# A state-space scan's read-outs summed and turned to token order in one step on TensorE

## The reference, cut to what matters

```
x = x + ssm(ctx, z=layernorm(x))       # z is read as (b, channel, time): the 256x256 of a sequence as it lies
x = x + ffn0(layernorm(x));  x = x + attention(layernorm(x), ctx);  x = x + ffn1(layernorm(x))

ssm:  u = silu(conv(in_proj_w @ ctx) + conv_b)          # 256 channels
      dt, B, C = x_proj_w @ u  (8, 16 and 16 rows);  delta = softplus(dt_proj_w @ dt + dt_proj_b)
      for every time t and state n:
          state[n] = state[n] * exp(delta * A[n]) + delta * u * B[n]
      y = sum_n state[n] * C[n]
      y = y + D * u
      y = y * silu(z)
      return y with channel and time swapped
```

## Time and profile before

| | before |
|---|---|
| median of 3 runs (lowest, highest) | 853.95 us (853.61, 855.42) |
| the profiled execution: its time, its span | 855.85 us, 853.9 us |
| TensorE matmul busy, share of the span | 728.4 us, 85% |
| VectorE busy | 600.3 us, 70% |
| ScalarE busy | 435.3 us, 51% |
| GpSimd busy | 292.6 us, 34% |
| mean granted TensorE clock | 0.909 |

### The profile page before, as it was taken

The page is one execution under the profiler, slowest core; times in us unless marked ns, Lnnn a source line. Parts: engine busy times, 40 slices in busy tenths (PEclk is TensorE's granted clock), DMA queues, the critical chain, the costliest instruction groups (busy, mean ns, idle before and its releaser), DMA issues.

```text
span 853.9 us, 10187 instructions
## 1 busy us (share of the span) xinstructions
PE 728.4 (85%) x3448; PEld 566.6 (66%) x3448; DVE 600.3 (70%) x1119; ACT 435.3 (51%) x836; POOL 292.6 (34%) x259
## 2 busy tenths in 40 slices
PE   5267636567868899999989999999899988999997
PEld 1012114345645678888789999998799876888886
DVE  6999986999999856645467566677656566455454
ACT  5555104555442354445467677766677645333342
POOL 0100321222233324445355555545354633212131
PEclk8575766888889999999989999999899999999999
DMA  6233321445354425455211111111111223433330
GB/s 178 98 107 103 113 78 55 114 131 165 121 167 113 124 74 172 148 163 162 70 53 41 34 59 32 50 44 33 26 51 56 75 79 99 144 117 101 103 130 25
DMA packets 40530, 81.33 MB, mean 95 GB/s; under 512 B 5752, under 2 KB 8064, under 8 KB 40480
## 3 DMA queue, kind: packets, MB, share of 16 engines
q1 hardware_dynamic: 40480, 80.69, 30.7%
HBM read 79.30 MB, written 1.38 MB: 94 GB/s over the span
## 4 chain that ended last, share of the span: by engine, by line
PE 56%; DVE 14%; issue 8%; ACT 4%; POOL 1%; DMA 0%; SPq 0%; DVEq 0%; ACTq 0%; POOLq 0%
PE bank L86 17%; PE bank L87 17%; PE bank L88 17%; PE bank L575 3%; DVE read_out L1030 3%; DVE state L1012 3%; DVE bank L1184 1%; DVE hidden_lo L914 1%; ACT probs L865 1%; DVE read_out L1038 1%; POOL probs L1429 1%; DVE bank L1187 1%; ACT w_hi L659 1%; PE bank L399 1%; DVE x_tok L1055 1%
## 5 line engine op out<-in xcount | busy, mean ns | idle before, releaser
L1376 POOL TENSOR_TENSOR w_lo<-w_raw,w_hi 128x768 fp32r<-128x768 f32 (+1 forms) x106 | 197.3, 1862 | 371.8 <-ACT w_hi L659 371.5
L86 PE MATMUL bank<-xt_hi,w_hi 128*128 128x512 f32 x400 | 169.2, 423 | 36.8 <-DVE hidden_lo L914 36.8
L659 ACT ACTIVATE w_hi<-w_raw 128x768 fp32r<-128x768 f32 (+1 forms) x106 | 85.7, 811 | 156.0 <-PE bank L88 125.0
L87 PE MATMUL bank<-xt_lo,w_hi 128*128 128x512 f32 x400 | 162.7, 407 | 0.0
L88 PE MATMUL bank<-xt_hi,w_lo 128*128 128x512 f32 x400 | 162.6, 407 | 0.0
L86 PEld LDWEIGHTS bank<-xt_hi,w_hi 128*128 128x128 f32 x400 | 77.9, 195 | 60.2 <-DVE hidden_lo L914 41.6
L659 ACT ACTIVATE hidden_hi<-bank 128x512 fp32r<-128x512 f32 x84 | 49.4, 588 | 121.7 <-DVE bank L1187 120.2
L369 PE MATMUL bank<-read_out,identity 128*128 128x512 f32 x96 | 64.0, 804 | 41.5 <-DVE read_out L1030 40.0
L914 DVE TENSOR_TENSOR hidden_lo<-bank,hidden_hi 128x512 fp32r<-128x512 f32 x84 | 57.8, 688 | 58.3 <-ACT hidden_hi L659 58.2
L1184 DVE TENSOR_TENSOR bank<-gated,bank 128x512 f32<-128x512 f32 x80 | 55.4, 692 | 50.7 <-PE bank L88 49.9
L88 PEld LDWEIGHTS bank<-xt_hi,w_lo 128*128 128x128 f32 x400 | 78.0, 195 | 19.3
(11 more groups left out here) (171 smaller groups left out, 1495.1 us busy)
## 6 DMA issues: line engine op xcount, KB each, us to landing
w_raw<-in_ffn_w SPq DMA_DIRECT2D x74, 384.0 KB, 3.3
b_rows<-bc_scratch SPq DMA_DIRECT2D x32, 256.0 KB, 3.6
c_rows<-bc_scratch SPq DMA_DIRECT2D x32, 256.0 KB, 3.2
route_bc<-route_scratch SPq DMA_DIRECT2D x32, 256.0 KB, 3.6
route_bc<-route_scratch SPq DMA_DIRECT2D x32, 192.0 KB, 3.3
w_raw<-in_attn_proj_w SPq DMA_DIRECT2D x16, 384.0 KB, 3.0
route_bc<-route_scratch SPq DMA_DIRECT2D x32, 128.0 KB, 3.7
w_raw<-in_attn_out_w SPq DMA_DIRECT2D x16, 256.0 KB, 2.6
```

The costliest lines, as they stand in the source:

```text
L86: e.matmul(out, w_hi, m_hi, start=first, stop=False)
L87: e.matmul(out, w_hi, m_lo, start=False, stop=False)
L659: e.activation(out, source, ACT.Copy).then_inc(sem(name), 1)
L1376: e.tensor_tensor(lo[:, 0:n], w_raw[p % RAW][:, 0:n], hi[:, 0:n].bitcast(F32), ALU.subtract).then_inc(sem("w_lo"), 1)
```

## The change

The sum over the states is made by transposes. `y_sum` now takes eight 128 x 128 blocks of a read-out and transposes each into bank 0 or 1 with accumulation, so that a bank holds one sequence in token order (2 x 128 tokens in turn, 256 channels), and y comes out turned. It runs once for each read-out in both halves; the pairs of half 1 are gone. D * u is made on ScalarE (`make_skip`) in slot 3 of `read_out` and is the first term of the sum (n = -1). z is transposed after it is normalised (`turn_z`, 16 transposes through banks 6 and 7), and silu reads it from PSUM into the place where z was, now in token order. After the sum VectorE multiplies the bank by z in place (`gate_y`) and adds it to x (`add_y`, which in half 1 follows in the same unit). `turn_y`, `add_pair` and `skip_and_gate` are gone.

```diff
--- before.py
+++ after.py
@@ -362,24 +362,30 @@
                     e.matmul(ps[:, :], dt_proj_sb[:, c * P:(c + 1) * P], x_dbl[0:DR, h * HT:(h + 1) * HT],
                              start=True, stop=True).then_inc(sem("dt"), 1)
 
-            def y_sum(h, n, tile, first):
-
-                for c in range(EH):
-                    ps = take(c, ("y_skip", 2 * h + c + 1)) if first else bank[c]
-                    last = e.matmul(ps[:, :], identity[:, :], tile[:, c, :], start=first, stop=n == DS - 1)
-                last.then_inc(sem(f"y_sum{h}"), 1)
-
-            def turn_y(h):
-                y = read_out[h]
+            def y_sum(h, n):
+
+                tile = read_out[3 if n < 0 else n % 4]
+                at.wait_ge(*(("skip", h + 1) if n < 0 else ("read", h * DS + n + 1)))
                 for b in range(HB):
-                    at.wait_ge("y_gated", 2 * h + b + 1)
-                    ps = misc(("y", h, b), ("y_added", 2 * h + b + 1))
+                    ps = take(b, ("y_added", 2 * h + b + 1)) if n < 0 else bank[b]
                     for l in range(SEQ // P):
                         for c in range(EH):
                             t = b * SEQ + l * P
-                            last = e.transpose(ps[:, l * DI + c * P:l * DI + (c + 1) * P], y[:, c, t:t + P],
-                                               identity[:, :])
-                    last.then_inc(sem("y_turn"), 1)
+                            last = e.matmul(ps[:, l * DI + c * P:l * DI + (c + 1) * P], tile[:, c, t:t + P],
+                                            identity[:, :], is_transpose=True, start=n < 0 and l + c == 0,
+                                            stop=n == DS - 1 and l + c == 2)
+                last.then_inc(sem(f"y_sum{h}"), 1)
+
+            def turn_z():
+
+                for b in range(BATCHES):
+                    at.wait_ge("z_norm", b // HB + 1)
+                    ps = take(6 + b % 2, ("z_gate", b + 1))
+                    for l in range(SEQ // P):
+                        for c in range(EH):
+                            last = e.transpose(ps[:, l * DI + c * P:l * DI + (c + 1) * P],
+                                               z_gate[:, b * EH + c, l * P:(l + 1) * P], identity[:, :])
+                    last.then_inc(sem("z_turn"), 1)
 
             def turn_acc(k, pair, ring=(0, 1)):
                 at.wait_ge("acc_copy0", k - 3)
@@ -478,14 +484,15 @@
             at.wait_ge("consts", 4)
             project_x_dbl(0)
             project_dt(0)
+            y_sum(0, -1)
             for n in range(DS):
-                at.wait_ge("read", n + 1)
-                y_sum(0, n, read_out[n % 4], n == 0)
+                y_sum(0, n)
+                if n == 1:
+                    turn_z()
                 if n == 2:
                     project_x_dbl(1)
                 if n == 6:
                     project_dt(1)
-            turn_y(0)
             for step in (5, 6, 7, 8, 11):
                 transition(2, step)
 
@@ -495,14 +502,8 @@
                 if u >= 2:
                     down(u - 2)
                 n = u + 1
-                if 2 < n < DS and n % 2 == 1:
-                    at.wait_ge("pair", (n - 1) // 2)
-                    y_sum(1, n - 2, read_out[(DS + 1 + n - 2) % 4], n == 3)
-                if n == DS + 1:
-                    at.wait_ge("pair", DS // 2)
-                    y_sum(1, DS - 1, read_out[(DS + 1 + DS - 1) % 4], False)
-                if n == DS + 2:
-                    turn_y(1)
+                if n <= DS + 1:
+                    y_sum(1, n - 2)
                 if n == DS + 4:
                     transition(3, 5)
                     transition(3, 6)
@@ -701,10 +702,21 @@
                                         ACT.Exp, scale=decay[:, c, n:n + 1])
                 last.then_inc(sem("decay"), 1)
 
-            def activate_z(h):
-                at.wait_ge("z_norm", h + 1)
-                z = z_gate[:, h * HC:(h + 1) * HC, :]
-                e.activation(z, z, ACT.Silu).then_inc(sem("z_gate"), 1)
+            def activate_z():
+                for b in range(BATCHES):
+                    at.wait_ge("z_turn", b + 1)
+                    e.activation(z_gate[:, b * EH:(b + 1) * EH, :].rearrange("p c s -> p (c s)"), bank[6 + b % 2][:, :],
+                                 ACT.Silu).then_inc(sem("z_gate"), 1)
+
+            def make_skip(h):
+
+                at.wait_ge("conv", 2 * HALVES)
+                if h > 0:
+                    at.wait_ge("y_sum0", DS + 1)
+                for c in range(EH):
+                    at.wait_ge("u", 2 * h + c + 1)
+                    last = e.activation(read_out[3][:, c, :], u_sb[:, h, c, :], ACT.Copy, scale=skip_d[:, c:c + 1])
+                last.then_inc(sem("skip"), 1)
 
             def round_weights(p):
                 if p >= PIECES:
@@ -786,12 +798,12 @@
             softplus_log(0)
             for n in range(4):
                 scan_decay(0, n)
+            make_skip(0)
             for n in range(DS):
                 if n + 4 < DS:
                     scan_decay(0, n + 4)
                 if n == 1:
-                    for h in range(HALVES):
-                        activate_z(h)
+                    activate_z()
                     for c in range(EH):
                         activate_u(1, c)
                 if n == 2:
@@ -804,6 +816,7 @@
                 round_weights(p)
             for step in (5, 6, 7, 8):
                 transition(2, step)
+            make_skip(1)
             for n in range(4):
                 scan_decay(1, n)
 
@@ -1016,39 +1029,20 @@
                 i = h * DS + n
                 at.wait_ge("state", i + 1)
                 at.wait_ge(f"ld_c{i % 3}", 16 * (i // 3 + 1))
-                if h == 0:
-                    slot = n % 4
-                    at.wait_ge("y_sum0", n - 3)
-                else:
-                    slot = (DS + 1 + n) % 4
-                    at.wait_ge("y_sum0", DS)
-                    if n == 3:
-                        at.wait_ge("y_turn", HB)
-                    elif n > 3:
-                        at.wait_ge("y_sum1", (n - 3) // 2)
-                        at.wait_ge("pair", (n - 2) // 2)
-                e.tensor_tensor(read_out[slot][:, :, :], state[i % 2][:, :, :],
+                at.wait_ge("y_sum0", n - 2 if h == 0 else DS + 1)
+                if h == 1:
+                    at.wait_ge("y_sum1", n - 2)
+                e.tensor_tensor(read_out[n % 4][:, :, :], state[i % 2][:, :, :],
                                 c_rows[i % 3][:, :].unsqueeze(1).broadcast_to([P, EH, HT]),
                                 ALU.mult).then_inc(sem("read"), 1)
 
-            def add_pair(n):
-
-                at.wait_ge("read", DS + n + 1)
-                both = read_out[(DS + 1 + n) % 4][:, :, :]
-                e.tensor_tensor(both, both, read_out[(DS + n) % 4][:, :, :], ALU.add).then_inc(sem("pair"), 1)
-
-            def skip_and_gate(h):
-                y = read_out[h]
-                at.wait_ge(f"y_sum{h}", DS if h == 0 else DS // 2)
-                for c in range(EH):
-                    e.scalar_tensor_tensor(out=y[:, c, :], in0=u_sb[:, h, c, :], scalar=skip_d[:, c:c + 1],
-                                           in1=bank[c][:, :], op0=ALU.mult, op1=ALU.add).then_inc(sem("y_skip"), 1)
-                at.wait_ge("y_skip", 2 * h + EH)
-                at.wait_ge("z_gate", h + 1)
-                z = z_gate[:, h * HC:(h + 1) * HC, :].rearrange("p (b c) s -> p c b s", c=EH)
+            def gate_y(h):
+                at.wait_ge(f"y_sum{h}", DS + 1)
                 for b in range(HB):
-                    y_b = y[:, :, b * SEQ:(b + 1) * SEQ]
-                    e.tensor_tensor(y_b, y_b, z[:, :, b, :], ALU.mult).then_inc(sem("y_gated"), 1)
+                    at.wait_ge("z_gate", h * HB + b + 1)
+                    t = h * HC + 2 * b
+                    e.tensor_tensor(bank[b][:, :], bank[b][:, :], z_gate[:, t:t + 2, :].rearrange("p t w -> p (t w)"),
+                                    ALU.mult).then_inc(sem("y_gated"), 1)
 
             def add_to_x(t, b, name, count):
                 two = x_tok[:, t:t + 2, :].rearrange("p t w -> p (t w)")
@@ -1057,8 +1051,8 @@
 
             def add_y(h):
                 for b in range(HB):
-                    at.wait_ge("y_turn", 2 * h + b + 1)
-                    add_to_x(h * HC + 2 * b, bank_of["y", h, b], "y_added", 2 * h + b + 1)
+                    at.wait_ge("y_gated", 2 * h + b + 1)
+                    add_to_x(h * HC + 2 * b, b, "y_added", 2 * h + b + 1)
                     for l in range(2):
                         chunk_stats(h, 2 * b + l)
                 find_variance(h)
@@ -1224,7 +1218,7 @@
                     normalise_z(1)
                 if n == 7:
                     softplus_floor(1)
-            skip_and_gate(0)
+            gate_y(0)
             add_y(0)
             softplus_excess(1)
             normalise_x(2)
@@ -1242,8 +1236,6 @@
             for u in range(U0):
```

(5 more changed lines are left out.)

## The result

| | before | after |
|---|---|---|
| median (lowest, highest; runs) | 853.99 us (853.61, 855.42; 4) | **842.73 us** (840.65, 844.82; 4) |
| profiled execution: its time, its span | 855.85, 853.9 us | 842.09, 840.1 us |
| TensorE, VectorE busy | 728.4, 600.3 us | 710.0, 587.8 us |
| mean granted TensorE clock | 0.909 | 0.905 |

The ratio is 0.9865, 95% interval 0.9837 to 0.9893: by it the kernel after is 11.5 us faster, between 9 and 14; the two medians are 11.3 us apart. The forecast was 842.6.

What follows compares the result with a forecast made beforehand. VectorE was taken to bound the kernel until 294 us, TensorE after. Gains of 0.5 + 1.5 + 6.4 + 2.9 = 11.3 us took 853.95 to 842.6 us; bounds 838.5 to 846.5, stated range 838 to 848.5.

Steps and rivals of the forecast that it cites:

- The bound: Before 294 us VectorE, not TensorE, is the bound; what it wins or loses there moves the end one for one.
- Transposes at the plain price: In the sums, eight accumulating transposes cost what plain ones do: 1.26 us hot, 1.97 us cold.
- Rival (c): In the sums, accumulating transposes cost fp32 passes with their own weight loads: about 850 us; chance 0.05.
- Shorter sum before project_dt(1): Sum ahead of that product falls from 2.51 to 1.97 us cold: 0.5 us gained, or 1.3 hot.
- End of half 0: From finished sum to first addition to x, 2.88 us becomes 1.35: 1.5 us gained.
- add_pair: Half 1: dropping eight pair sums gives 7.9 + 0.4 us, less 1.9 for read-outs held by GpSimd: 6.4 us gained.
- End of half 1: Multiply-adds and gate, 4.37 us, become 1.44: 2.9 us gained.
- Off the path: ScalarE's make_skip copies (0.6 us each) and z activations delay nothing; make_skip(1) costs 1.2 us once if uncovered.
- (a): Rival: TensorE takes over in half 1 at a mixed clock, 6 us lost, 848.6 us; chance 0.09.
- (b): Rival whose wording the text leaves out; counted under slower than 853.95 us; chance 0.04.
- (d): Rival: half 1's read-outs are not stalled by GpSimd in six units, 8.3 us more, 834.3 us; chance 0.06.
- The bounds: Whole kernel: the forecast time lies within 838.5 to 846.5 us, chance 0.72.

Runs made afterwards that it cites:

- e4: Kernel after, with GpSimd writing zeros for the low parts of sixteen weight pieces instead of subtracting: 822.14 us, ratio 0.9624.
- e6: Kernel after, half 1's read-out moved ahead of rest_hidden and GpSimd's subtraction waiting for it in units 1 to 14: 821.60 us; 819.68 when run again.
- after_again: The kernel after, unchanged, run again beside the kernel before (853.55 us): 844.35 us, ratio 0.9892.
- e9: Kernel before without add_pair, old sums kept, read-out ahead of rest_hidden and GpSimd waiting for it: 822.11 us; 821.92 when run again.
- e1: Kernel before without add_pair in half 1, each read-out summed alone by the old fp32 products: 844.96 us, ratio 0.9883.
- e3: Kernel after with every set of eight accumulating transposes made twice: 841.76 us, ratio 0.9857.
- e8: e6 with GpSimd's subtractions for rest-weight blocks 0 to 3 also made to wait, around the end of half 0: 816.27 us, ratio 0.9538.
- e7: Kernel after with GpSimd's subtraction waiting for the unit's read-out, VectorE's order kept: 831.07 us, ratio 0.9724.

## Why the prediction was right, step by step

- **The bound.** VectorE decides up to the turn of x, and what it wins moves the end one for one. Right: 12.4 us at the turn, 11.3 between the medians. e4 confirms it with 20.6 us at the turn and 20.6 between its median and that of the kernel after, which did not run beside it; e6 with 20.3 and 22.8 (against after_again, which ran beside it).
- **Transposes at the plain price.** Right: 1.97 us at a granted clock of 0.50, 1.03 to 1.09 at 1.00; the forecast calls these levels 1.2 and 2.4 GHz, an estimate that fits two products of 512 columns 0.42 us apart at 0.50, 1.2 columns a ns. The 1.26 us that I took for hot, also at 1.00, were too many; the earlier trace rows had a set of 1.10. Rival (c) falls with it.
- **Shorter sum before project_dt(1), 0.5 us.** 0.5, cold, as taken. That the new sums would be cold in half 0 was my estimate, which no row of the kernel before shows; the kernel after had a granted clock of 0.50 from 60 to 72 us and from 73 to 113 us. e9 shows what the term left out: at a clock of 0.72 and 0.86 in the same stretch the old sums are not behind at all.
- **End of half 0, 1.5 us.** 1.7: it took 1.20 us from the gate to the first addition, not 1.35, and the wait for the sum was 2.06 us instead of 2.13.
- **add_pair, 6.4 us.** 7.2, of which the route rows took back 0.6. e1, alone, gave 7.45. The additions and the collision that moves to the read-out were right in kind; the term that was mis-sized is the read-out's stall, 1.25 us (2.46 less 1.21) and not 1.38. Six times the 0.13 us between them is the missing 0.8.
- **End of half 1, 2.9 us.** 3.1. Right as a sum, and the earlier trace rows had shown the held gate product. e9 shows that 1.4 of it was a collision that goes, which the text counted as part of the edit without saying that any other cure would take it too.
- **Off the path.** `make_skip` took 0.71 us for each copy, not 0.6:

```profile
L718 ACT ACTIVATE read_out<-u_sb,small_sb x4: 705/705/705, 33.7 to 134.3; 128x512 f32<-128x512 f32 x4
```

  (shortest, median and longest in ns.) Neither it nor `activate_z` is in VectorE's waits. What I didn't have was the 0.6 us more for the route rows (5.3 us against 4.7). That isn't the edit's: in after_again, the same kernel, the wait was 4.6 us. The transfers are issued sooner too (143.4 against 146.2 us), and took 4.0 us to land here, 3.6 in the kernel before and in after_again.
- **The rivals.** (a) and (b), the slower ones: the mean clock in half 1 was 0.85, and e3, with twice the transposes, shows that there was room. Whether transposes themselves keep the clock up was open: in the second part of half 0 it was 0.50 with eight a step (kernel after) and 0.66 with sixteen (e3). So transposes can raise the clock, and eight a step did not. (d) did not happen by itself. e6 made it happen, and it is worth more than (d)'s 8.3 us, since the drives are freed too.
- **What GpSimd holds.** `gate_y`'s products, with one operand in PSUM, were not held: 1.30 and 1.29 us for the two, the second time with a subtraction that starts beside them, at 269.26 us. But an operand pair in SBUF isn't the only case: e8 shows normalising instructions with one large SBUF operand that were held (2.74 against 1.38 us).
- **The agreement of 842.73 with 842.6 is better than the method.** By the turns the gain was 12.4 us and by the two profiled executions 13.8, of which 1.4 lie where TensorE is the bound. The medians gave 11.3, and 9.2 when both ran again (853.55 against 844.35). The forecast was a gain of 11.3 at the turn, so there it was 1.1 us short, of which 0.3 is the start of the trace; that the medians gave just 11.3 is luck. Within this spread, errors of 0.3 to 0.8 us in the terms can't be told from the clock's.
- **The bounds.** The prediction names 838.5 to 846.5 and doesn't work them out. Its own bounds on the read-out's stall (+6.4 and -4.7 us, where it took -1.9) would by themselves reach from 834.3 to 845.4. The result lay near the middle and doesn't test them.

## What to carry to other kernels

A reduction that one engine does in front of another (adding pairs so that TensorE sums half as often) should go as soon as the engine behind has idle time; it was worth 7.5 of 12.4 us by itself. Before rewriting a stage, look for instructions of one shape with two durations: here they were 1.2 and 2.8 us, the other engine's instruction ended 1.1 us before the long one's end each time, and giving that engine a wait and a place beside PSUM work was worth more than the rewrite (20.3 us at the turn against 12.4). And price an edit a second time without the collision it avoids, since 1.4 of the 3.1 us at the end of half 1 came with either cure.

## What the runs showed of the hardware that I had not expected

- **Transposes alone can raise TensorE's clock.** Sixteen per step of the scan: granted clock 0.66 in the second part of half 0, from 0.50 (80 to 85 us) to 0.95 (95 to 100 us) inside it (e3); eight: 0.50 (kernel after). VectorE's wait before the gate of half 0 was 2.06 us in both, with twice the work in e3.
- **The scan instruction is held by GpSimd too**, 2.83 instead of 2.28 us (e7), when the subtraction's last 0.7 us fall into it. The subtraction that starts beside instructions with an operand in PSUM isn't slowed by them (1.83 to 1.86 us) nor they by it (0.69).
- **One large SBUF operand is enough in one case.** The four normalising instructions took 2.74 us beside subtractions and 1.38 without (e8).
- **The GpSimd instruction that only writes didn't hold VectorE.** In e4 eight sets of zeros lie beside a drive, which takes its short time all the same (GpSimd's spans are rough, but each set follows at once on the `w_hi` that it waits for), where a subtraction beside a drive made it 2.76 us (kernel after):

```profile
189.91 1.20 DVE L1016 TENSOR_TENSOR drive<-delta_u,b_rows 128x1024 f32<-128x1024 f32 x1
...
189.71 0.74 POOL L1368 MEMSET w_lo<- 128x768 f32 x1 [4.21 <-ACT w_hi L660]
```

  In these runs it is GpSimd's reading, or its two operands, that counts; which of the two wasn't tried.
